# GpSimd's state fade moved ahead of its indirect DMAs, and the shared unit moved ahead of the expert tile's step in each quarter of a chunk

## The reference, cut to what matters

```python
# state-space part: 64 heads of 8, state 128, chunks of 128 tokens
y = causal_conv_silu(xBC); cum = cumsum(dt * A)            # within a chunk
Yd = einsum(CB * exp(cum_i - cum_j) * dt, xs)              # near and far in the chunk
S  = S * exp(cum_last) + states(chunk)                     # state, chunk after chunk
y  = Yd + exp(cum) * C @ S_before + D * xs
out1 = rmsnorm(y * silu(z)) * norm_w @ W_out.T
# expert part: 8 experts of 128, the 2 best of each token, and a shared unit of 512
combine = top2(softmax(x @ w_gate))
routed = sum_e combine_e * (silu(x @ Wg_e) * (x @ Wu_e)) @ Wd_e
shared = (silu(x @ Wsg) * (x @ Wsu)) @ Wsd
x = x + out1 + routed + shared
```

## Time and profile before

| | |
|---|---|
| three timed runs | 1494.15, 1502.84 (median), 1506.90 us |
| the profiled execution | 1498.83 us, its span 1497.1 us |
| mean granted clock of PE over the span | 0.938 of full speed |
| busy over the span | PE 1286.0 us (86%), DVE 885.9 (59%), ACT 567.9 (38%), POOL 354.7 (24%) |
| busy from 80 to 587 us (chunks of the first layer) | PE 423.0 of 507.0 us |

### The profile page before, as it was taken

One profiled execution on the slowest core, in us unless ns is written; L12 is line 12 of the kernel. 1 busy time (PEld: TensorE's weight loads), 2 busy tenths in 40 slices (PEclk: granted clock), 3 DMA queues, 4 the chain that ended last, 5 costly groups with the idle time before them and its releaser, 6 DMA issues. The chain is left out here.

```text
span 1497.1 us, 21861 instructions
## 1 busy us (share of the span) xinstructions
PE 1286.0 (86%) x7439; PEld 804.8 (54%) x7443; DVE 885.9 (59%) x1723; ACT 567.9 (38%) x957; POOL 354.7 (24%) x344
## 2 busy tenths in 40 slices
PE   5677988998988687999999998999766989998987
PEld 3334646654664455666666644454543456544564
DVE  5767566556656585543224379889777453556334
ACT  2474476547647551222222242443312313223311
POOL 3186031221302522510301002221037000000045
PEclk9788999999999888999999999999857999999999
DMA  9142123122211412300000150000002100111123
GB/s 360 55 139 84 47 60 96 50 54 71 79 41 35 132 51 97 103 1 0 0 0 0 68 186 0 1 0 1 2 28 85 31 28 29 36 43 57 57 58 111
DMA packets 72082, 88.87 MB, mean 59 GB/s; under 512 B 19174, under 2 KB 55334, under 8 KB 71337
## 3 DMA queue, kind: packets, MB, share of 16 engines
q1 hardware_dynamic: 65836, 70.78, 15.1%
q0 software_dynamic: 6144, 16.79, 3.5%
HBM read 61.14 MB, written 26.38 MB: 58 GB/s over the span
## 5 line engine op out<-in xcount | busy, mean ns | idle before, releaser
L414 PE MATMUL l_banks<-l_xnT,all_region_a 128*128 128x512 f32 x288 | 133.7, 612 | 5.6 <-ACTq L805 4.8
L2019 PE MATMUL l_banks<-l_xnT,mid_region_c 128*128 128x512 f32 (+1 forms) x192 | 89.6, 617 | 10.8 <-DVE l_xnT L2235 10.8
L970 POOL TENSOR_TENSOR all_region_b<-all_region_b,l_lc 128x512 f32<-128x512 f32 x64 | 88.2, 1398 | 31.5 <-DMA all_region_b<-l_lc_rows 31.2
L414 PEld LDWEIGHTS l_banks<-l_xnT,all_region_a 128*128 128x128 f32 x288 | 55.0, 197 | 65.9 <-issue 55.5
L794 ACT ACTIVATE all_region_b<-all_region_b 128x512 f32<-128x512 f32 x64 | 69.5, 1087 | 17.9 <-PE l_banks L414 14.0
L414 PE MATMUL l_banks<-all_region_a,all_xa 128*128 x234 | 68.7, 411 | 6.9 <-DVE all_x L1041 5.4
L1200 DVE SCALAR_TENSOR_TENSOR l_xbc<-l_pre,all_cols,l_xbc 128x512 f32<-128x512 f32 x72 | 61.7, 857 | 19.2 <-ACT l_xbc L727 14.2
L2019 PEld LDWEIGHTS l_banks<-l_xnT,mid_region_c 128*128 128x128 f32 (+1 forms) x192 | 35.2, 189 | 57.3 <-issue 45.4
L962 POOL TENSOR_TENSOR l_yr<-l_yr,all_neg_half 128x1 f32<-128x1 f32 x16 | 10.3, 643 | 232.7 <-DVE l_yr L1063 232.7
L2902 POOL TENSOR_TENSOR l_rstd<-l_moments,all_neg_half 128x4 f32<-128x4 f32 x12 | 12.4, 1032 | 220.8 <-DVE l_moments L2962 220.8
L1257 DVE TENSOR_TENSOR all_region_b<-all_region_b,l_cbd 128x512 f32<-128x512 f32 x64 | 59.0, 924 | 7.6 <-ACT all_region_b L794 3.9
(11 more groups left out here) (475 smaller groups left out, 2854.6 us busy)
## 6 DMA issues: line engine op xcount, KB each, us to landing
all_region_b<-l_lc_rows SPq DMA_DIRECT2D x256, 64.0 KB, 2.0
all_xa<-slots_in SPq DMA_DIRECT2D x39, 128.0 KB, 2.1
slots_out<-all_xa SPq DMA_DIRECT2D x39, 128.0 KB, 2.1
mid_vector_rows<-slots_in SPq DMA_DIRECT2D x39, 128.0 KB, 2.1
slots_out<-all_region_a SPq DMA_DIRECT2D x39, 128.0 KB, 1.7
slots_in<-l_xp SPq DMA_DIRECT2D x4, 1024.0 KB, 12.8
all_region_a<-l_gate_up SPq DMA_DIRECT2D x1, 4096.0 KB, 15.8
all_x<-x SPq DMA_DIRECT2D x4, 512.0 KB, 5.7
```

The costliest lines, as they stand in the source:

```text
L414: return nc.tensor.matmul(out, lhsT, rhs, start=start, stop=stop, **kw)
L970: nc.gpsimd.tensor_tensor(bc[:, k, :, :], bc[:, k, :, :], spread(lc[:, c, heads], 1, BLK), ALU.subtract).then_inc(dd_ready.sem, 1)
L2019: return nc.tensor.matmul(out, lhsT, rhs, start=start, stop=stop)
```

## The change

**POOL.** In every chunk `fade` now comes directly behind the previous chunk's `differences`, ahead of any scatter or fetch. The scatters of group 0 are dealt out anew (2 and 6, 8, 8 in place of 4, 6, 4 and 4, 6 behind the first eight), and the 8 fetches of group 3 stand behind `differences(3, 2)`. **DVE.** The adds of the fetched rows move from the middle of chunk (3, 1) to its end (tiles 0 and 1) and to the middle of chunk (3, 2) (tiles 2 and 3), and `measure(0)` from the end of chunk (3, 1) to the third quarter of (3, 2). **PE, ACT, DVE and the bank order.** In a quarter the unit's piece now comes first, then the tile's step as `th`, `gu`, `dn`, `tx`. On ACT the read-out of `gu` comes ahead of that of `dn`. SP's order is the same as before, and no instruction is added or removed.

```diff
     def tile_jobs(f):
-        work = ((("dn", f - 4), 4), (("gu", f - 1), 6), (("th", f - 3), 5), (("tx", f), 5))
+        work = ((("th", f - 3), 5), (("gu", f - 1), 6), (("dn", f - 4), 4), (("tx", f), 5))
...
                 fs = steps_at.get((g, c, k), [])
-                for f in fs[:1]:
-                    order += tile_jobs(f)
                 if (c, k) in unit_at:
                     name, n = unit_at[c, k]
                     order.append(((name, g, n), 4))
-                for f in fs[1:]:
+                for f in fs:
                     order += tile_jobs(f)
...
-                    tiles = steps_at.get((g, c, k), [])
-                    for f in tiles[:1]:
-                        tile_step(f)
                     if (c, k) in unit_at:
                         name, n = unit_at[c, k]
                         if name == "up":
                             half_unit(g, name, n)
                         else:
                             down(g, n)
-                    for f in tiles[:1]:
-                        tile_turn(f)
-                    for f in tiles[1:]:
+                    for f in steps_at.get((g, c, k), []):
                         tile_step(f)
-                        tile_turn(f)
...
         def tile_step(f):
 
-            if 0 <= f - 4 < MOE_TILES:
-                i = f - 4
-                jobs.wait_room(pe, 0, ("dn", i))
-                pe.wait_ge(hT_ready.sem, hT_ready.done(0, i))
...
                 jobs.fill(last, ("gu", i))
                 owner_of(i + 1)
-
-        def tile_turn(f):
-
+            if 0 <= f - 4 < MOE_TILES:
+                i = f - 4
+                jobs.wait_room(pe, 0, ("dn", i))
+                pe.wait_ge(hT_ready.sem, hT_ready.done(0, i))
...
-        late = {0: ((6,), (7, 8)), 1: ((9, 10), (11, 12)), 2: ((13, 14, 15), ())}
+        late = {0: ((4,), (5, 6, 7)), 1: ((), (8, 9, 10, 11)), 2: ((), (12, 13, 14, 15))}
         for g in range(GROUPS):
             if g == 0:
                 for t in range(GT):
                     scatter(t)
             differences(g, 0)
-            if g == 0:
-                for t in range(GT, GT + 2):
+            for c in range(NCH):
+                fade(g, c)
+                ahead, behind = late.get(c, ((), ())) if g == 0 else ((), ())
+                for t in ahead:
                     scatter(t)
-            for c in range(NCH):
+                if c + 1 < NCH:
+                    differences(g, c + 1)
+                for t in behind:
+                    scatter(t)
                 if (g, c) == (GROUPS - 1, 1):
                     for t in range(GT):
                         fetch(t)
-                fade(g, c)
-                ahead, behind = late.get(c, ((), ())) if g == 0 else ((), ())
-                if c + 1 < NCH:
-                    differences(g, c + 1)
-                    for t in ahead:
-                        scatter(t)
                 if c > 0:
                     out_scale(g, c - 1)
-                for t in behind:
-                    scatter(t)
...
         def tiles_and_unit(g, c, k):
 
-            tiles = steps_at.get((g, c, k), [])
-            for f in tiles[:1]:
-                tile_step(f)
             unit_step(g, c, k)
-            for f in tiles[1:]:
+            for f in steps_at.get((g, c, k), []):
                 tile_step(f)
...
                 tiles_and_unit(g, c, 1)
-                if (g, c) == (GROUPS - 1, 1):
-                    add(0)
-                    add(1)
+                if (g, c) == (GROUPS - 1, 2):
+                    add(2)
+                    add(3)
...
                 tiles_and_unit(g, c, 2)
-                if (g, c) == (GROUPS - 1, 1):
-                    add(2)
-                    add(3)
+                if (g, c) == (GROUPS - 1, 2):
+                    measure(0)
...
                 if (g, c) == (GROUPS - 1, 1):
-                    measure(0)
+                    add(0)
+                    add(1)
```

More of the change, by code:

```diff
@@ L484, in tile_step @@
         def tile_step(f):
-            if 0 <= f - 4 < MOE_TILES:
-                i = f - 4
-                jobs.wait_room(pe, 0, ("dn", i))
-                pe.wait_ge(hT_ready.sem, hT_ready.done(0, i))
-                part = w.down[:, bass.ds(expert[i] + SHARED, 1), :]
-                jobs.fill(mm(jobs.bank(("dn", i))[:, 0:DIM], hmT[i % 2], part.rearrange("p a n -> p (a n)")), ("dn", i))
             if 0 <= f - 3 < MOE_TILES:
@@ L508, in tile_step @@
                 owner_of(i + 1)
-        def tile_turn(f):
+            if 0 <= f - 4 < MOE_TILES:
+                i = f - 4
+                jobs.wait_room(pe, 0, ("dn", i))
+                pe.wait_ge(hT_ready.sem, hT_ready.done(0, i))
+                part = w.down[:, bass.ds(expert[i] + SHARED, 1), :]
+                jobs.fill(mm(jobs.bank(("dn", i))[:, 0:DIM], hmT[i % 2], part.rearrange("p a n -> p (a n)")), ("dn", i))
             if f < MOE_TILES:
@@ L797, in tile_step @@
         def tile_step(f):
+            if 0 <= f - 1 < MOE_TILES:
+                i = f - 1
+                jobs.wait_filled(act, 0, ("gu", i))
+                if i >= 2:
+                    act.wait_ge(h_ready.sem, h_ready.done(0, i - 2))
+                nc.scalar.activation(tanh[:, i % 2, :], jobs.bank(("gu", i))[:, 0:P], ACT.Tanh, scale=0.5).then_inc(
+                    s_ready.sem, 1)
             if 0 <= f - 4 < MOE_TILES:
@@ L805, in tile_step @@
                 jobs.free(act.drain(), ("dn", i))
-            if 0 <= f - 1 < MOE_TILES:
-                i = f - 1
-                jobs.wait_filled(act, 0, ("gu", i))
-                if i >= 2:
-                    act.wait_ge(h_ready.sem, h_ready.done(0, i - 2))
-                nc.scalar.activation(tanh[:, i % 2, :], jobs.bank(("gu", i))[:, 0:P], ACT.Tanh, scale=0.5).then_inc(
-                    s_ready.sem, 1)
             if f < MOE_TILES:
```

## The result

The changed kernel takes **1503.76 us** (median of 20 runs, 1499.06 to 1506.75); the kernel before, beside it, 1497.95 us (20 runs, 1494.15 to 1506.90). The ratio is 1.0029 (95% interval 1.0016 to 1.0041): a little slower, where 1484 was forecast, and above the range of 1472 to 1501. The profiled execution of after has a span of 1502.0 us.

The account below looks back on a forecast made before the run. PE, busy 86% of the span, was taken as the bound, so only its standstills can give time. -17 + 4.4 - 7 + 3 = -16.6 gave 1484 us; own range 1476 to 1493, wider range 1472 to 1501.

Parts of the forecast that it names:

- A: Chunk (3, 1): the fade ahead of the fetches starts at once, ending PE's long idle and slow clock, -17 us.
- the rows of 4.56 and 0.93: DVE's `near` took 4.56 us behind late fades, 0.93 behind a prompt one; the forecast took 0.93 for chunk (3, 1).
- B: Chunk (3, 2): the adds and measure put there lengthen it by +4.4 us, range 2 to 5.
- C: Chunk (0, 2): the fade starts earlier and PE's 6.22 us idle goes, -7 us, range 5 to 8.
- D: New quarter order: last quarters +7 us over seven chunks, less smaller waits elsewhere, sum +3, range -2 to +6.
- `tx` at 285.24 + 1.4 = 286.6, +1.0: Last quarters: add, release and `dn` now stand between DVE's `near` and `tx`, delaying PE by 1.0 us a chunk.
- -2.5 for first quarters: First quarters of (2, 0) and (3, 0): PE's waits for ACT's late read-out go since the piece runs first, -2.5 us.
- -1.5 for the others: First to third quarters: other PE waits for ACT and the unit's add shrink by 1.5 us.
- Rival 3: `dn` waits in all 28 quarters, up to 1.2 us each, 34 in all: 1515 us, slower than before; chance 0.07.
- The rule: From the skill: two-input VectorE and GpSimd lock a shared port per instruction, so `near` waits for one difference, never four.

Follow-up runs that it names:

- adds_late: fades_only with adds 2 and 3 and the measure moved from chunk (3, 2) to (3, 3): 1485.45 us, 0.9910 of the kernel before.
- own_sem: fades_only with the first four tiles' scatters counted on their own semaphore, so normalising group 1 waits for them alone: 1483.45 us, 0.9895 of before.
- g3_only: Only the change's group 3 part (fade ahead of fetches, adds and measure moved) put on the kernel before: 1488.51 us, 0.9915 of before.
- fades_only: The change without its new quarter order; POOL's new order and the moved adds and measure kept: 1484.68 us, 0.9893 of before.
- quarter_only: Only the change's new quarter order on PE, ACT and DVE, put on the kernel before: 1516.99 us, 1.0111 of before.
- fill_wait: The whole change, with three unread 128x512 products filling PE's wait ahead of `dn` in four last quarters: 1494.04 us, 0.9963 of before.
- last_old: The whole change, but the last quarter of every chunk keeps the old order: 1487.05 us, 0.9900 of before.
- best_c2: The change plus `weigh` and `near` last, adds, measure, first quantising in (3, 3), separate scatter semaphore, one tile's scatters earlier: 1507.12 us, 0.9908 of before, chip kind B.

## Why the prediction was wrong

- **A, right.** -16.7 for -17; the fade at once, `near` 0.93. The choice between the rows of 4.56 and 0.93 was the right one.
- **B, too small.** +6.6 for +4.4, outside of its own range of 2 to 5. The sum had only DVE's instructions. In (3, 2) PE waits 2.1 and 1.15 us for DVE and then runs at a lower clock; adds_late shows that all of it hangs on this work.
- **C, right in its chunk and wrong for the kernel.** (0, 2) gave -7.6 for -7. The step "The last scatter goes out a little earlier than before, so SP's first tile rows and the normalising of group 1 aren't late" failed in its second half. The scatter does start 0.8 us earlier, counted from chunk (0, 0), but PE and DVE come 8.9 us earlier, so they now wait for it, and (0, 3) gives 6.8 back. own_sem shows both waits. g3_only against fades_only leaves about 3 us.
- **D, the step that decided.** +3 was forecast; measured were some 20 us (after against fades_only) or 17 (quarter_only, 0.0111 of 1501), 14.5 to 16.1 of it in (1, 0) to (3, 0). "`tx` at 285.24 + 1.4 = 286.6, +1.0" was right: fill_wait leaves 0.9 to 1.1 a chunk. What the term left out is that the products behind a stand of 2.6 us run at a granted clock of 0.60, 1.6 to 3.2 us more per chunk (after against fill_wait), 9.6 in four chunks. Another 4.4 us over fades_only stand in (3, 0) and 2.0 in (0, 3); these were not taken apart. What the term took as credits, -2.5 for first quarters and -1.5 for the others, does not show in the chunks: (3, 0) is 4.5 longer, (2, 0) 0.7 shorter.
- **Rival 3** put the loss in all 28 quarters; it stands in the last ones (last_old), but for (3, 0), where PE waits 1.56 us ahead of `dn` in the second quarter. That a loss of its kind would outweigh the fades was right; its place and its size (34 us for 17 to 20) were not. The text said that the forecast is wrong if chunks of groups 1 and 2 change by over 1.5 us each; four of the six with pieces did.
- The Trainium skill ("SBUF — State Buffer", "Who interferes with whom") gave the right end of term A. But what it says does not hold in every row. Timeline of DVE, then of POOL, in best_c2:

```profile
526.54 4.68 DVE L1350 SCALAR_TENSOR_TENSOR all_x<-all_xa,all_share,all_x 128x256 f32<-128x256 f32 x4
```

```profile
527.07 1.06 POOL L1007 TENSOR_TENSOR l_st<-l_st,l_total 128x512 f32<-128x512 f32 x1
528.10 5.48 POOL L997 TENSOR_TENSOR all_region_b<-all_region_b,l_lc 128x512 f32<-128x512 f32 x4
```

The adds that took 2.19 us took 4.68 beside GpSimd's fade and differences, and PE waited 5.59 us behind them; the same kernel had 2.19 in its other profile. The rule would give one GpSimd instruction at a time.

## What to carry to other kernels

Price a wait of the matmul engine twice: its length, and what its clock costs the products behind it. Two waits of 1.0 and 0.4 us were followed by a slow clock in 8 of 40 quarters here, one of 2.6 in 12 of 12. If such a wait can't go, work that nobody reads can be cheaper than standing still (0.66% of this kernel). When two read-outs share banks with the work of the same quarter, look at what the reading engine does ahead of both; moving one of them only renames the wait. And before counting a gain, look for the next event whose time is fixed by another queue (here the 32nd scatter).
